# Tap 8 computed in chunks 1 to 7, steps moved between engines, and TensorE's column halves, in a dynamic convolution followed by a deformable one

## The reference

```
x = x + conv0(gn(x))
x = x + conv1(gn(x))
```

## Time and profile before

| | |
|---|---|
| median of three runs | 5768.44 us (5765.39 to 5774.8) |
| the profiled execution | 5764.16 us, its span 5762.4 us |
[...]
| PE / DVE / ACT / POOL busy | 81% / 80% / 38% / 71% |
| gathers | 4308 |

### The profile page before, as it was taken

One profiled execution on the slowest core, in us unless ns is written; L12 is line 12 of the kernel. 1 busy time (PEld: TensorE's weight loads), 2 busy tenths in 40 slices (PEclk: granted clock), 3 DMA queues, 4 the chain that ended last, 5 costly groups with the idle time before them and its releaser, 6 DMA issues.

```text
span 5762.4 us, 38546 instructions
## 1 busy us (share of the span) xinstructions
PE 4653.8 (81%) x11780; PEld 1745.7 (30%) x11780; DVE 4582.5 (80%) x5064; ACT 2165.7 (38%) x3057; POOL 4105.2 (71%) x4315
## 2 busy tenths in 40 slices
PE   7576888978879788787887878788897887988783
PEld 3122332323323233232332323233232332323231
DVE  5978969789696886969879697886978979688664
ACT  3333434343343433434434344343433434343320
POOL 1777677776767767677776777767777677776776
PEclk8777888978789787888988889788887888978895
DMA  3334353343534435344343443434334353433433
GB/s 97 106 121 132 99 139 109 117 131 104 142 95 131 122 106 138 94 132 118 111 136 94 132 117 114 134 98 139 109 116 130 97 146 101 129 114 106 123 108 101
DMA packets 281823, 675.11 MB, mean 117 GB/s; under 512 B 77119, under 2 KB 116618, under 8 KB 279370
## 3 DMA queue, kind: packets, MB, share of 16 engines
q0 software_dynamic: 206784, 564.93, 33.2%
q1 hardware_dynamic: 74832, 107.71, 7.4%
HBM read 618.23 MB, written 54.12 MB: 117 GB/s over the span
## 4 chain that ended last, share of the span: by engine, by line
PE 57%; DVE 28%; POOL 6%; issue 5%; ACT 2%; DMA 1%; POOLq 0%; DVEq 0%; ACTq 0%; SPq 0%
PE yo_ps L733 15%; PE z_ps L672 8%; PE conv_ps L630 7%; DVE pairs L1280 6%; DVE conv_ps L1171 6%; POOL gat L493 6%; DVE gat L1301 6%; PE yo_ps L630 5%; PE tap_ps L663 4%; PE z_ps L739 4%; PE conv_ps L553 3%; PE z_ps L671 3%; PE xh_ps L638 2%; DVE stat L1197 1%; DVE xb L1195 1%
## 5 line engine op out<-in xcount | busy, mean ns | idle before, releaser
L493 POOL DMA_INDIRECT gat<-patch_table,ixu x4308 | 4097.2, 951 | 1643.5 <-issue 1268.0
L1301 DVE TENSOR_TENSOR gat<-gat,wgt_ps 128x1024 f32<-128x1024 f32 x1077 | 1305.1, 1214 | 553.4 <-DMA gat<-patch_table,ixu 546.6
L733 PE MATMUL yo_ps<-hat_s,hat_image 128*128 128x512 f32 x3000 | 1398.0, 614 | 8.7 <-DVE hat_wy L1335 8.7
L1280 DVE TENSOR_REDUCE pairs<-gat 128x256 f32<-128x1024 f32 x1024 | 1240.2, 1211 | 0.0
L663 PE MATMUL tap_ps<-ident,pairs 128*128 128x128 f32 x2048 | 398.2, 326 | 838.1 <-DVE pairs L1280 838.1
L973 ACT ACTIVATE val<-tap_ps 128x512 f32<-128x512 f32 x512 | 304.6, 595 | 1439.2 <-PE tap_ps L663 1438.2
L733 PEld LDWEIGHTS yo_ps<-hat_s,hat_image 128*128 128x128 f32 x3000 | 562.5, 196 | 821.2 <-issue 734.5
L672 PE MATMUL z_ps<-val,w_pair 128*64 128x512 f32 x1024 | 668.0, 752 | 13.6 <-ACT val L973 13.6
L663 PEld LDWEIGHTS tap_ps<-ident,pairs 128*128 128x128 f32 x2048 | 262.1, 162 | 1217.9 <-DVE pairs L1280 1033.8
L1171 DVE SCALAR_TENSOR_TENSOR conv_ps<-xh,kb,conv_ps 128x1024 f32<-128x1024 f32 x480 | 617.8, 1287 | 12.7
L1335 DVE TENSOR_TENSOR hat_wy<-yo_ps,hat_wy 128x512 f32<-128x512 f32 x300 | 206.6, 689 | 250.7 <-PE yo_ps L733 248.0
(11 more groups left out here) (219 smaller groups left out, 4304.9 us busy)
## 6 DMA issues: line engine op xcount, KB each, us to landing
gat<-patch_table,ixu POOLq DMA_INDIRECT x4308, 2.7
xb<-in_x SPq DMA_DIRECT2D x31, 1024.0 KB, 9.7
patch_table<-rec SPq DMA_DIRECT2D x120, 256.0 KB, 2.3
hat_image<-patch_table SPq DMA_DIRECT2D x135, 128.0 KB, 4.6
out<-n_z SPq DMA_DIRECT2D x128, 128.0 KB
patch_table<-np SPq DMA_DIRECT2D x2, 1072.5 KB
patch_table<-gat SPq DMA_DIRECT2D x8, 256.0 KB, 2.2
patch_table<-rec SPq DMA_DIRECT2D x16, 97.0 KB
```

The costliest lines, as they stand in the source:

```text
L493: pool.indirect_dma_start(gat[:, k, t * 2 * REC:(t + 1) * 2 * REC], None, table_rows, bass.IndirectOffsetOnAxis(ixu[:, i, k, t:t + 1], 0)) ...
L733: m = pe.matmul(hat_sum[:, :], hat_image[:, i, t, :], hat_s[:, i, :], start=(i == 0), stop=(i == HI - 1))
L1280: dve.tensor_reduce(total, gat[:, k, :].rearrange("p (t x c h) -> p t c x h", t=TILES, x=2, h=2), mybir.AxisListType.XY, ALU.add).then_inc ...
L1301: dve.tensor_tensor(patch, patch, wk.rearrange("p (n h) -> p n h", h=2).unsqueeze(2).to_broadcast([128, TILES * 2, C, 2]), ALU.mult).then_ ...
```

## The change

It does seven things. (1) `HATS` becomes chunks 1 to 7 for images 1 to 15, and chunks 3 to 7 (`HATS0`) for image 0; before it was chunks 0 to 4, and none in image 0. The hat image is loaded for image 0 too, and for later ones behind output 6. (2) `x_stats` moves from chunks 0 to 3 to chunks 5 and 6; the chain that makes the nine taps (`x_mean` to `kernels`) moves from chunk 4 to chunk 7; `points` comes in two halves of four chunks, in chunks 6 and 7. (3) The clip at 20 goes from DVE to ACT, as `Relu(20 - u)` followed by `Exp(20 - ...)`; the normalisation of the lower 64 partitions and, for images after the second, that of `hidden`'s input go from DVE to ACT. (4) `offsets_two` computes the offsets of two chunks in one bank, one on output partitions 0 to 40, the other on 64 to 104, with alternating matmuls; two chunks' pixels share `om_ps`. (5) `to_z` makes each product into z of 512 columns two of 256, the second on output partitions 64 to 127; SiLU then has two halves. (6) `last_row`, the group statistics and `to_pixels` use other banks (`tr_ps`, `om_ps`, `yo_ps`) than `xh_ps`; `to_pixels` waits for the latest `hat_post`, and the following `hat_up` for the copy out of `yo_ps`. (7) `hat_post 0` goes from unit 2 to unit 3.

```diff
-HATS = (0, 1, 2, 3, 4)
+HATS0 = (3, 4, 5, 6, 7)
+HATS = (1, 2, 3, 4, 5, 6, 7)
...
-PLAN_FIRST = ((2, "convolve 0"), (3, "convolve 1"), (5, "convolve 2"), (6, "exp"), (7, "ln"), (7, "x_stats"), (8, "tanh"))
+PLAN_FIRST = ((2, "convolve 0"), (3, "convolve 1"), (5, "convolve 2"), (6, "exp"), (7, "ln"), (8, "tanh"))
...
+PLAN_NORM = ((1, "project"), (3, "residual"), (4, "group_mean"), (5, "group_var"), (6, "normalise"), (8, "finish"))
 PLAN_PREPARE = (
+    ((1, "last_row"), (1, "offsets 0"), (2, "to_table 0"), (2, "x_stats 0"), (3, "to_pixels 0"), (3, "to_table 1"), (4, "offsets 1"),
+     (4, "to_table 2"), (5, "x_stats 1"), (6, "to_table 3"), (7, "to_pixels 1"), (8, "to_table 4"), (8, "finish")),
+    ((1, "offsets 2"), (2, "to_table 5"), (2, "points 0"), (3, "to_pixels 2"), (4, "points 1"), (4, "offsets 3"), (4, "to_table 6"),
+     (5, "x_stats 2"), (6, "points 2"), (6, "to_table 7"), (7, "to_pixels 3"), (7, "x_stats 3"), (8, "finish")),
+    ((1, "x_mean"), (1, "points 3"), (2, "x_var"), (2, "points 4"), (2, "next_indices"), (3, "x_norm"), (3, "points 5"),
+     (4, "hidden_units"), (5, "kernel_taps"), (6, "kernels"), (6, "hidden 0"), (7, "hidden 1"), (8, "hidden 2"), (8, "finish"), (KK, "hidden 3")),
 )
-PLAN_HAT = ((1, "hat_rows"), (1, "hat_up 0"), (2, "hat_post 0"), (3, "hat_up 1"), ...
+PLAN_HAT = ((1, "hat_rows"), (1, "hat_up 0"), (3, "hat_post 0"), (3, "hat_up 1"), ...
...
-    return NCH <= q < B * NCH and q % NCH in HATS
+    return q < B * NCH and q % NCH in (HATS if q >= NCH else HATS0)
...
         # SP
-                store_out(b, 5)
+                for g in range(5, NCH - 1):
+                    store_out(b, g)
                 if more:
                     load_hat_image(b + 1)
-                for g in range(6, NCH):
-                    store_out(b, g)
+                store_out(b, NCH - 1)
...
         # PE
+            def offsets_two(n, s):
+                if s == 0:
+                    pe.wait_ge(np_done, n * 2 + 2)
+                else:
+                    pe.wait_ge(om_done, n * NCH + s * 2)
+                for i in range(6):
+                    for j in range(2):
+                        m = pe.matmul(om_ps[C * j:C * j + OM, :], w_om[:, i, :], inner(np1, 0, 128, (s * 2 + j) * ROWS + 2 * (i // 3), i % 3),
+                                      start=(i == 0), stop=(i == 5))
+                m.then_inc(om_mm, 2)
...
             def to_pixels(n, s):
                 pe.wait_ge(om_done, n * NCH + s * 2 + 2)
+                if n > 0 and ups[0]:
+                    pe.wait_ge(hat_scaled, ups[0])
...
+            def to_z(weights, columns, start=False, stop=False):
+                for j in range(2):
+                    m = pe.matmul(z_ps[C * j:C * j + C, 0:CH // 2], weights, columns[:, j * CH // 2:(j + 1) * CH // 2], start=start, stop=stop)
+                return m
...
             def hat_up(q, t):
+                if after_px:
+                    pe.wait_ge(px_done, after_px.pop())
+                ups[0] = HT * h + t + 1
...
         # ACT
             def hidden(n, s):
+                    for j in range(2):
+                        act.wait_ge(xh_mm, n * NCH + s * 2 + (j + 1))
+                        act.activation(n0[C:, j, :], xb[C:, n % 2, span(s * 2 + j)], ACT.Identity, bias=mr0[C:, 2:3],
+                                       scale=mr0[C:, 1:2]).then_inc(n0_done, 1)
...
             def exp(n, s, buf=0):
+                    act.wait_ge(conv_sum, (n - 1) * CONV_SUMS + s * KK + KK)
+                    act.activation(u[:, :, :].rearrange("p j c -> p (j c)"), conv2_ps[:, :], ACT.Relu, bias=twenty, scale=-1.0).then_inc(clip, 2)
...
-                act.activation(zs[:, :], z_ps[0:C, :], ACT.Silu, bias=bn_shift[:, :], scale=bn_scale[:, :]).then_inc(zs_done, 1)
+                for j in range(2):
+                    m = act.activation(zs[:, j * CH // 2:(j + 1) * CH // 2], z_ps[C * j:C * j + C, 0:CH // 2], ACT.Silu,
+                                       bias=bn_shift[C * j:C * j + C, :], scale=bn_scale[C * j:C * j + C, :])
...
         # DVE
             def points(n, part):
-                points_of(n, part, math, n * MATH_STEPS, 0, NCH)
+                half = part // 3
+                points_of(n, part % 3, math, (n * 2 + half) * MATH_STEPS, half * NCH // 2, NCH // 2)
```

More of the change, by code:

```diff
@@ L63 @@
     ((1, "project"), (3, "residual"), (3, "convolve 0"), (4, "convolve 1"), (5, "convolve 2"), (6, "exp"), (6, "first_points 4"),
-     (7, "ln"), (7, "x_stats"), (8, "tanh"), (8, "finish")),
+     (7, "ln"), (8, "tanh"), (8, "finish")),
 )
-PLAN_NORM = ((1, "project"), (3, "residual"), (4, "x_mean"), (4, "group_mean"), (5, "x_var"), (6, "group_var"), (6, "x_norm"),
-             (7, "hidden_units"), (8, "kernel_taps"), (8, "finish"), (8, "normalise"), (KK, "kernels"))
+PLAN_NORM = ((1, "project"), (3, "residual"), (4, "group_mean"), (5, "group_var"), (6, "normalise"), (8, "finish"))
@@ L76 @@
 )
-PLAN_HAT = ((1, "hat_rows"), (1, "hat_up 0"), (2, "hat_post 0"), (3, "hat_up 1"), (5, "hat_post 1"), (5, "hat_out 0"), (5, "hat_up 2"),
+PLAN_HAT = ((1, "hat_rows"), (1, "hat_up 0"), (3, "hat_post 0"), (3, "hat_up 1"), (5, "hat_post 1"), (5, "hat_out 0"), (5, "hat_up 2"),
             (6, "hat_out 1"), (7, "hat_post 2"), (7, "hat_up 3"), (8, "hat_out 2"), (KK, "hat_post 3"))
@@ L670, in product @@
                     rows = slice(side(q // NCH), side(q // NCH) + OM)
-                    pe.matmul(z_ps[0:C, :], w_cat[rows, :], cat[rows, span(q % NCH)], start=True, stop=False)
-                pe.matmul(z_ps[0:C, :], w_pair[:, p, :], val[:, p % 2, :], start=False, stop=False)
+                    to_z(w_cat[rows, :], cat[rows, span(q % NCH)], start=True)
+                to_z(w_pair[:, p, :], val[:, p % 2, :])
             def last_products(b, g):
@@ L738, in hat_out @@
                 pe.wait_ge(hat_scaled, HT * hats_before(q) + t + 1)
-                pe.matmul(z_ps[0:C, :], w_hat[:, :], hat_wy[:, t, :], start=False, stop=False).then_inc(hat_used, 1)
+                to_z(w_hat[:, :], hat_wy[:, t, :]).then_inc(hat_used, 1)
             pe.wait_ge(x_first, 16)
@@ L1054, in image @@
                          "next_indices": lambda b, g, i: next_indices(b + 1),
[L1055 removed]
+                         "offsets": lambda b, g, i: offsets_two(b + 1, i), "to_pixels": lambda b, g, i: to_pixels(b + 1, i)} if more else {}
                 if b == 0:
@@ L1412, in image @@
                 if further:
-                    steps["hidden"] = lambda b, g, i: hidden(b + 2, i)
-                    steps["x_stats"] = lambda b, g, i: x_stats(b + 2, g)
+                    steps["x_stats"] = lambda b, g, i: x_stats(b + 2, i)
                     steps["x_mean"] = lambda b, g, i: x_mean(b + 2)
```

148 lines of the change are left out of this document (84 added, 64 removed).

## The result

The changed kernel takes 6122.15 us (median of four runs, 6065.33 to 6132.74) where the kernel before takes 5768.55 us: a ratio of 1.059 [1.0525, 1.0658]. It is slower, as forecast, but by 354 us and not by 112, and outside the range (5600 to 6010). The profiled execution took 6132.74 us, its span 6130.9; its mean granted TensorE clock was 0.827 of the full one, where the kernel before had 0.833.

A forecast was written before the change was run, and what follows sets the result against it. Gather issue on POOL was taken to pace the kernel before. Chunk terms 37 + 3 x 44.3 + 35.5 + 108 + 48 gave 361.4 us an image against 352.9; 5762.4 + 110 + 20 + 10 - 28 = 5874, forecast 5880, range 5600 to 6010.

The forecast's parts named there:

- The halves of the offsets: Chunks 5 and 6: two chunks' offsets on two column halves overlap, 5.4 us a pair, bounds 5.4 and 10.4.
- The rival of the halves: Offsets and products: halves do not overlap, 6225 us, or halfway, weight loads of 0.12 in line, 6050; chance 0.12.
- 0.43 us an offset instruction: Offsets in chunks 5 and 6: lower bound, all but the first instruction pair up, 12.5 x 0.43 = 5.4 us.
- A product into z: Every chunk: four half-length instructions instead of 1.0 us, forecast 0.78 us, bounds 0.64 and 1.07.
- The wait for `om_done`: Chunks 5 and 6: `to_pixels 0` right behind `offsets 0` waits for ScalarE's steps, 3.1 us not covered by transposes.
- The moves on the queues: SP queue: the hat image's ten loads move behind `store_out 6`; next user 37 us later, load lands in 4.6: nothing.
- The last image: No convolution there, POOL sets it: 8 gathers fewer, -10, and POOL starting up to 18 us further ahead: -28.
- 1.8 three times (bounds 0 and 4 x 2.4): 5.4: Chunks 5 and 6: slower clock behind `to_pixels`, from small matmuls and idle time, adds 5.4 us an image.
- 1.5 for a cold start: Chunk 7: 1.5 us added to PE's three `hat_up` of 13.5 us, within the chunk's 48 us.
- chunks 1 to 3: A DVE-PE-DVE chain binds; clip, wait, products and `x_stats` save 3.2 us: 47.5 becomes 44.3 each.
- The two products into z inside the chain shrink (below): -0.5: Chunks 1 to 3: half-size products shorten the binding chain by 0.5 us a chunk.
- PE's order fits and POOL paces again: Whole kernel: waits and clock put in partly vanish; 5640 us at half the waits, 5340 with none; faster, chance 0.25.

The follow-up runs named there:

- Experiment 5: Changed kernel plus unused matmuls in TensorE's idle time, at more places than in experiment 1: 5857.26 us, 1.0155 to the kernel before.
- Experiment 2: Changed kernel with `hat_post 0` moved back from unit 3 to unit 2: 6134.67 us, 1.0646 to the kernel before.
- experiment 8: Kernel before with only the half-size products into z and SiLU in two halves: 5751.41 us, 0.9971 to the kernel before.
- experiment 3: Also `z_whole`: changed kernel with each product into z whole again (512 columns) and one SiLU: 6131.38 us, 1.0636 to the kernel before.
- experiment 1: Changed kernel plus unused matmuls ahead of some `hat_up` and `to_pixels` steps: 6037.32 us, 1.0475 to the kernel before.
- experiment 9: Kernel before plus seven unused matmuls ahead of the second transposes in chunks 1 to 3 of images 1 to 14: 5725.62 us, 0.991.
- hats_1to5: Changed kernel with hat chunks 1 to 5 only and none in image 0: 5604.38 us, 0.9718 to the kernel before.

## Why the prediction was off

**Right.** The direction, and the reason for it: the gathers stop pacing, and chunks 5 and 6 are nearly full of PE (49 us busy of 54 and 55). Chunk 0 (37 forecast, 37.3), chunk 4 (35.5, 35.8). The halves of the offsets overlap fully (5.4 forecast, 5.35). The rival of the halves falls in both of its forms: 24 instructions take 5.35 us where twelve took 5.31, 0.04 more, where 24 weight loads of 0.12 in the line would be 2.8. The 0.43 us an offset instruction in the forecast's bounds stands in no row; the twelve of the kernel before took 0.44 each (5.31/12), the 24 of the changed kernel 0.22. A product into z takes 0.65 us at a grant of 1.00 and not 0.78. The wait for `om_done` (3.26 us, forecast 3.1) and that for `yo_ps` (0.59, forecast 0.4) cost what was said, and POOL waits 54 us an image, over 30. The moves on the queues cost nothing that the trace shows: PE waits for no load of the hat image, its one wait for a DMA being 6.1 us for `xb` at the start. The last image took 314.8 where 338.7 - 28 = 310.7 was forecast.

**The term that failed is the clock.** The text put "1.8 three times (bounds 0 and 4 x 2.4): 5.4" into chunks 5 and 6 and "1.5 for a cold start" into chunk 7, and nothing into chunks 1 to 3: 6.9 us an image. Experiment 5 gives at least 20.1. Of the 17.2 us by which an image missed the forecast, at least 13.2 are thus the clock. The rest, 4.0, is the difference between this run and the forecast without clock (358.5 and 361.4 - 6.9 = 354.5): 2.6 in chunks 1 to 3 and parts of a microsecond elsewhere. It need not be a further error of the forecast: DVE's 3.4 us in chunk 1 behind the fillers are more than the 2.6, and `hat_up 0` of chunks 3 and 4 was still late. By size:

- chunks 1 to 3: 8.2 over the forecast, 5.6 of it gone with the fillers;
- chunks 5 and 6: 5.0 over, and 10.5 gone with the fillers, where 5.4 had been put in and even the upper bound was 9.6;
- chunk 7: 3.4 over, 4.4 gone;
- image 0 took 385.8 for 369 and image 14 362.7 for 351; with the fillers they take 375.5 and 349.0.

Together 13 x 17.2 + 17 + 12 + 4 = 257 us, and 5874 + 257 = 6131, the span.

**How the step went wrong.** The step is the one that priced the clock by new idle time alone. The forecast took the durations of `hat_up` from rows at the full clock (4.56 us, at a grant of 1.00) and asked only where new idle time would stand. It didn't ask which instruction would be the first behind idle time that was there already. In the kernel before, PE idled for some 7 us in chunks 1 to 3 too, and short work behind it carried the loss. PE's timeline in chunk 2 of its sixth image:

```profile
2021.12 1.11 PE L663 MATMUL tap_ps<-ident,pairs 128*128 128x128 f32 x4 [7.08 <-DVE pairs L1280]
...
2024.06 1.97 PE L672 MATMUL z_ps<-val,w_pair 128*64 128x512 f32 x2
...
2027.48 4.56 PE L733 MATMUL yo_ps<-hat_s,hat_image 128*128 128x512 f32 x10
```

The product takes 1.97 us for 1.07, and `hat_up 2` behind it 4.56. The granted clock was 0.51 from 2022.16 to 2027.4 us, over the products, and 1.00 over this `hat_up`. The change lays `hat_up 1` behind that idle stretch, and its half-size products leave 2.19 us idle ahead of `hat_up 2`. A late `hat_up` costs up to 3 us, and where DVE is there first, it waits. The same sum counted a gain, "The two products into z inside the chain shrink (below): -0.5", and missed that what they give is idle time on PE. Experiment 2 shows that the move of `hat_post 0` alone is not the cause: undone, the idle time and the loss show at another place for the same total. The half-size products do make `hat_up 2` late, in the kernel before too (experiment 8), but with whole ones the image is as long (experiment 3). Experiments 1 and 5 show that work in the idle time helps, in chunks 1 to 3 only once the idle time ahead of the transposes was filled too (141.8 us with the fillers of experiment 1 and 135.5 with those of 5, 141.1 with none).

**The rival "PE's order fits and POOL paces again"** was wrong for seven hat chunks even with the clock kept up at most places (358.5 us an image); with five POOL does pace (340.6).

## What to carry to other kernels

When a step is moved or shortened on TensorE, list what stands idle in front of each long group of matmuls afterwards, not only the idle time that is new: here idle time cost little in front of short products (filling it gave 2.7 us an image, experiment 9), and it made a ten-instruction group that another engine waits for up to 3 us longer (7.47 us for 4.56 behind 6.53 us of it, 7.60 behind 2.19). Test it with unused matmuls in the idle time; if more work makes the kernel faster (here 5857 us for 6122) and the long groups fall back to their shorter time (4.65 us for 5.70), the clock is the term. Put them at every place that idles: behind a stretch of 3.34 us that was left, four instructions took 3.78 us themselves, at a grant of 0.50, and held the chain (experiment 1). And before chasing it, take off load until the intended bound paces: five hat chunks gave 5604 us at a mean grant of 0.772, where seven with fillers gave 5857 at 0.923.

## What was not expected of the hardware

- Alternating matmuls on the two column halves, 41 output partitions each, took 5.35 us for 24 instructions, and the same 24 grouped by half 8.82, both at a grant of 1.00.
- A stretch of 2.19 us without work ahead of `hat_up 2` went with 7.60 us for it, one of 0.92 us (`z_whole`) with 4.56. But in `hats_1to5` a `hat_up 2` behind 2.19 us took 4.56 in some chunks and 7.56 in others, so the length of one idle stretch doesn't settle it.
- The mean granted clock does not order the kernels by time: 0.772 goes with 5604 us, 0.809 with 5751, 0.827 and 0.866 with 6122 and 6131, 0.923 with 5857.
